# A fused feed-forward and attention block: in the first stage the two half products of a token tile walk together

## The reference

```python
x = x + 0.5 * ffn(layernorm(x))      # first layer
x = x + attention(layernorm(x))      # 32 heads, 8 key/value heads, per token
x = x + 0.5 * ffn(layernorm(x))      # third layer, the same weights

def ffn(x):                          # 1024 -> 1024, 64 centroids
    dots = softmax(x @ centroids.T / 0.1)
    hits = dots > 0.01
    query_sel, cluster_sel = any(hits, axis=1), any(hits, axis=0)
    dense = x @ weight.T + bias
    return where(query_sel[:, None] & cluster_sel[assignments][None, :], dense, 0)
```

## Time and profile before

| | us |
|---|---|
| median of 3 runs | 1223.47 (1221.32 to 1224.46) |
| span of the profiled execution, first to last instruction | 1220.6 |
| PE busy | 1207.2 (99%) |
| PE weight loads busy | 1039.3 (85%) |
| DVE busy | 858.3 (70%) |
| ACT busy | 412.6 (34%) |
| POOL busy | 420.5 (34%) |

### The profile page before, as it was taken

One profiled execution on the slowest core, in us unless ns is written; L12 is line 12 of the kernel. 1 busy time (PEld: TensorE's weight loads), 2 busy tenths in 40 slices (PEclk: granted clock), 3 DMA queues, 4 the chain that ended last, 5 costly groups with the idle time before them and its releaser, 6 DMA issues.

```text
span 1220.6 us, 21763 instructions
## 1 busy us (share of the span) xinstructions
PE 1207.2 (99%) x8536; PEld 1039.3 (85%) x8536; DVE 858.3 (70%) x1272; ACT 412.6 (34%) x590; POOL 420.5 (34%) x551
## 2 busy tenths in 40 slices
PE   7999999999999999999999999999999999999998
PEld 6888888888888888888888888888888888888887
DVE  6644654554463587888878888788888874289897
ACT  5322232222121234444444444444434443212120
POOL 1344445444226443233333333333233200050322
PEclk9999999999999999999999999999999999999999
DMA  8577767775754456555565555555555555117885
GB/s 275 148 198 243 200 196 208 226 205 163 202 135 167 110 132 177 148 153 136 156 164 139 153 151 154 156 140 159 135 169 141 137 151 183 38 54 248 302 288 194
DMA packets 318982, 208.54 MB, mean 171 GB/s; under 512 B 258336, under 2 KB 281632, under 8 KB 318880
## 3 DMA queue, kind: packets, MB, share of 16 engines
q1 hardware_dynamic: 303712, 187.74, 53.5%
q10 hardware_dynamic: 15168, 19.40, 4.7%
HBM read 118.49 MB, written 88.60 MB: 170 GB/s over the span
## 4 chain that ended last, share of the span: by engine, by line
PE 79%; DVE 7%; DMA 7%; issue 3%; SPq 2%; POOL 1%; ACT 1%; POOLq 0%; DVEq 0%; ACTq 0%
PE ps_b L276 12%; PE ps_b L278 12%; PE ps_b L277 12%; PE ps_a L276 9%; PE ps_a L278 9%; PE ps_a L277 9%; PE ps_t L283 5%; PE ps_s L1406 4%; PE ps_s L290 2%; DMA late<-x_scratch 2%; PE ps_s L292 2%; PE ps_s L1451 2%; DMA qkv_scratch<-qkv_tok 1%; DMA y_scratch<-xa 1%; DVE late L1188 1%
## 5 line engine op out<-in xcount | busy, mean ns | idle before, releaser
L276 PE MATMUL ps_a<-w_hi,odd_hi 128*128 128x512 f32 (+1 forms) x472 | 187.6, 397 | 0.0
L278 PE MATMUL ps_a<-w_hi,odd_lo 128*128 128x512 f32 (+1 forms) x472 | 183.5, 389 | 0.0
L277 PE MATMUL ps_a<-w_lo,odd_hi 128*128 128x512 f32 (+1 forms) x472 | 183.0, 388 | 0.0
L276 PE MATMUL ps_b<-proj_hi,y_hi 128*128 128x256 f32 (+1 forms) x512 | 177.7, 347 | 0.0
L278 PE MATMUL ps_b<-proj_hi,y_lo 128*128 128x256 f32 (+1 forms) x512 | 172.7, 337 | 0.0
L277 PE MATMUL ps_b<-proj_lo,y_hi 128*128 128x256 f32 (+1 forms) x512 | 172.0, 336 | 0.0
L309 POOL TENSOR_TENSOR var_eps<-moments,eps 128x1 f32<-128x1 f32 x96 | 18.4, 191 | 394.9 <-DVE moments L305 394.9
L684 POOL TENSOR_TENSOR x_ring<-x_ring,f_tmp 128x1024 f32<-128x1024 f32 x32 | 77.1, 2410 | 156.4 <-DVE probs L1139 112.7
L989 DVE TENSOR_TENSOR f_out<-ps_b,bias_a 128x512 f32<-128x512 f32 x30 | 20.7, 691 | 140.5 <-PE ps_b L278 140.4
L632 POOL TENSOR_SCALAR f_out<-f_out,token_on 128x1024 f32<-128x1024 f32 x30 | 85.6, 2855 | 75.8 <-DVE f_out L989 75.6
L278 PEld LDWEIGHTS ps_b<-proj_hi,y_lo 128*128 128x128 f32 x512 | 97.1, 190 | 10.8
(11 more groups left out here) (192 smaller groups left out, 2726.1 us busy)
## 6 DMA issues: line engine op xcount, KB each, us to landing
xa<-in_L_attn_x SPq DMA_DIRECT2D x32, 512.0 KB, 5.0
f_tmp<-f_scratch SPq DMA_DIRECT2D x32, 512.0 KB, 4.5
x_ring<-in_L_attn_x SPq DMA_DIRECT2D x32, 512.0 KB, 3.4
f_scratch<-f_out SPq DMA_DIRECT2D x30, 512.0 KB, 3.9
x_scratch<-x_ring SPq DMA_DIRECT2D x30, 512.0 KB, 3.2
y_scratch<-xa SPq DMA_DIRECT2D x28, 512.0 KB, 4.3
ya_tok<-y_scratch SPq DMA_DIRECT2D x112, 128.0 KB, 3.3
late<-x_scratch SPq DMA_DIRECT2D x22, 512.0 KB, 6.9
```

Source lines behind the costliest of these rows:

```text
L276: pe.matmul(acc, hi[:, k, :], w_h[:, k, cols], start=(k == 0), stop=False)
L277: pe.matmul(acc, hi[:, k, :], w_l[:, k, cols], start=False, stop=False)
L278: last = pe.matmul(acc, lo[:, k, :], w_h[:, k, cols], start=False, stop=(k == KB - 1))
```

## The change

A new function, `product_whole(t)`, does both halves of a tile in one walk over the 8 blocks. Each of the three stationary blocks of a step is used for half 0 and then for half 1, so that successive matmuls write two banks in turn, and the walk waits for both `f1_read[0]` and `f1_read[1]` before its first matmul. `ffn1[0]` is raised by the last matmul but one and `ffn1[1]` by the last. The walk takes the place of both halves for tiles 2p and 2p+1 with p from 2 to 12: 22 tiles, 1056 matmuls. The other tiles, and all other engines' programs, stay as they were.

```diff
+                def product_whole(t, between={}):
+                    hi, lo = first_set(t)
+                    acc = first_acc(t)
+                    pe.wait_ge(lo1, t + 1)
+                    for h in range(2):
+                        pe.wait_ge(f1_read[h], t - 1)
+                    for k in range(KB):
+                        if k in between:
+                            between[k]()
+                        for n, (x, w) in enumerate(((hi, w_hi), (hi, w_lo), (lo, w_hi))):
+                            for h in range(2):
+                                last = pe.matmul(acc[:, half(h)], x[:, k, :], w[:, k, half(h)],
+                                                 start=(k == 0 and n == 0), stop=(k == KB - 1 and n == 2))
+                                if k == KB - 1 and n == 2:
+                                    last.then_inc(ffn1[h], 1)
...
                 for p in range(1, NP - 2):
-                    product_first(2 * p, 0, {3 if p == 1 else 1: lambda: fold_pair(p)})
-                    product_first(2 * p, 1)
+                    if p == 1 or p == NP - 3:
+                        product_first(2 * p, 0, {3 if p == 1 else 1: lambda: fold_pair(p)})
+                        product_first(2 * p, 1)
+                    else:
+                        product_whole(2 * p, {1: lambda: fold_pair(p)})
                     if p > 1:
                         pair_first(p + 1)
-                    product_first(2 * p + 1, 0)
                     if p == 1:
+                        product_first(2 * p + 1, 0)
                         pair_first(p + 1)
-                    if p < NP - 3:
                         product_first(2 * p + 1, 1)
+                    elif p < NP - 3:
+                        product_whole(2 * p + 1)
+                    else:
+                        product_first(2 * p + 1, 0)
```

## The result

The changed kernel takes 1242.45 us (median of 4 runs, 1241.67 to 1242.68) against 1223.72 us of the kernel before; the ratio is 1.0156, with a 95% interval of 1.0141 to 1.0170. It is slower by 18.7 us. The profiled execution has a span of 1240.8 us and took 1242.68 us.

The account below looks back on a forecast made before the run. PE bounds the kernel as a nearly hole-free row of matmuls. Eleven later `pair_first`, 10 x 1.97 + 0.94 = 20.6 us, take the span from 1220.6 to 1241.2; 2.9 us around it give 1244 us, range 1230 to 1252.

Parts of the forecast that it names:

- The stream: PE's 1056 matmuls in the two-bank walk: the step stays 0.2265 us, 0 gained or lost by repeated block or bank change.
- The rivals with a faster stream: PE's matmul step gets shorter: 13.9 us back, 1230 us (chance 0.10), or enough to win, 1203 us (chance 0.04).
- the 131 ns of the Trainium skill: Skill's time per sustained 512-column matmul on PE; it would gain 101 us, but the prediction held the trace's 226.5 ns against it.
- The stall: PE at `pair_first`: low part queued behind DVE's late read, start 1.87 us later plus 0.10 us exposed weight load, 1.97 us each.
- The first of the eleven: First affected `pair_first`, behind tile 4, where PE already waited: starts at 84.75 instead of 83.81, 0.94 us more.
- The sum: First stage, eleven `pair_first` for p = 2 to 12: 10 x 1.97 + 0.94 = 20.6 us more.
- Behind the first stage: Later stages: PE waits for hardly anything, no wait could shrink, so the loss stays and everything shifts by 20 us.
- The span and what lies around it: Whole execution: span 1220.6 + 20.6 = 1241.2 us, plus 2.9 us around it as before, 1244 us.
- The 1.7 us to spare: ACT's high part ends at 154.62, low part not wanted before 156.30; a longer stall, 1252 us, had chance 0.09.
- The clock: Rival: PE's clock falls to 1.2 GHz for a tile after ten 1.7 us holes, 96 us, 1340 us; chance 0.03.

Follow-up runs that it names:

- the low part ahead of the read: The changed kernel with one swap on DVE, low part of tile 2p+3 before the read of half 0 of tile 2p: 1222.50 us, ratio 0.9999.
- the read ahead: The changed kernel with the read of half 1 of tile 2p also moved before the low part of tile 2p+3 on DVE: 1260.62 us, ratio 1.0310.
- the halves, again: Repeat of the kernel before with the pair's centroid product moved behind the sixth block of half 0 of tile 2p+1: 1221.97 us, ratio 0.9984.

## Why the prediction was right

The forecast was 1244 us, 20 us slower, and 1242.45 us was measured; the spans are 1241.2 forecast and 1240.8 measured. Step by step:

- **The stream.** Forecast: no gain from the repeated block, none from the change of bank. Shown: 0.2268 us a step after, as many weight loads, and equal times, to within their intervals, with the walk and without it once the signal is the same (1242.02 in halves, 1242.45 whole). The rivals with a faster stream fall, and with them the 131 ns of the Trainium skill ("TensorE: Matmul & The Clock Gate", "Back-to-back issue gap").
- **The stall.** Forecast 1.87 us per `pair_first` and 0.10 us for the exposed load; measured 1.86 us, and 0.22 us to the second matmul. DVE's read was forecast 0.02 us ahead of the end of the tile's last step and started 0.02 us ahead of it (161.14 against 161.16).
- **The first of the eleven.** Forecast 0.94 us more than before; measured 0.91 (from the centroid product ahead of it 20.36 us against 19.45).
- **The sum.** Forecast 20.6 us for the first stage. Measured between the third and the last centroid product: 323.49 us (64.97 to 388.46) against 302.67 (64.36 to 367.03), so 20.8. The 0.2 us that the sum lacks are a wait at the last centroid product, at 388.46, of a tile behind the changed ones, which was not considered: the row of its weight load shows 0.46 us idle, until L967.
- **Behind the first stage.** The prediction had the rest merely shifted. From the last centroid product to the end of the span it took 852.3 us against 853.6: 1.3 us less. The 1.9 us wait at 462 us, which the profile of before shows, is not in the profile after, which has one of 0.4 us at 918 us instead. No profile with a late report of the even tiles has that wait; the prediction counted on no wait that could shrink, and there was one. The medians too differ by 2.1 us less (18.7) than the first stage lost in the profiles (20.8).
- **The span and what lies around it.** The spans agree to 0.4 us, and that is in part luck: the third centroid product, ahead of every changed tile, already came 0.6 us later (64.97 against 64.36), the first stage lost 0.2 us more than forecast, and 1.3 us came back behind it. From span to time 2.9 us were given; in the recorded executions with both numbers it is 1.8 to 1.9. So about 1 us of the 2.9 is that the profiled execution of before was a short one of its kernel, and this and the 0.4 us are most of the 1.6 us by which 1244 came out high.
- **The 1.7 us to spare.** Held: in all eleven pairs the low part followed the read at once, without a wait for its turn or for ACT. In the pair shown the high part was ready 1.95 us ahead of it (159.80 and 161.75), where 1.7 was forecast. With the low part ahead of the read this spare time is gone, and some pairs waited for the DMA round trip.
- **The clock.** Given 0.03 and it did not fall, behind eleven holes of 1.7 us. The reason given was weak: one hole of 1.9 us without a fall. With the read ahead there is a hole of the same 1.9 us that has a fall behind it, while one of 2.3 us in the halves, again (at 461 us), has none. That none of the eleven of 1.7 us had one was right, by a margin that nobody knew then. The price of the rival was far off: a fall costs 1.5 us and not the 9.6 us of a whole tile. The change of bank moved the clock nowhere: with the low part ahead of the read all eleven executions show 1.00.

## What to carry to other kernels

When two results of an engine are reported together instead of one after the other, look at who reads the first, and at what stands behind that read on the reader's in-order queue: here a read moved by half a tile held up work that PE needed 0.22 us after it was ready. An engine that is 70% busy can still be without slack at one place of its order. The cheap repair, both ways of which brought the time back here, is to put what the bound engine waits for ahead of what only waits for the bound engine, or to give the bound engine other work first.

## What the runs showed of the hardware

- Using one 128x128 fp32r block for two matmuls running saves nothing inside the stream: each matmul has its own weight load of 188 ns, and the step is 0.2268 us in two alternating banks, 0.2265 us in one.
- The granted clock stayed at 1.00 (2.4 GHz) behind eleven holes of 1.7 us on PE in the profile, and its mean at 1.00 in all four executions. With eleven holes of 2.3 us and one of 1.9 us it went to 1.2 GHz for about 3 us behind 7 of the 12, every second one and the last, which is the one of 1.9 us; with one hole of 4.0 us and ten of 3.15 us behind 4 of these 11; each fall cost about 1.5 us. So the longer holes had fewer falls, and the time does not go up evenly with the hole: 0.6 us more per hole cost 18 us in all, another 0.9 us per hole only 5. The length of a hole alone does not decide it: the hole of 1.9 us in the kernel before had no fall, that of 2.3 us in the halves with the pair product inside had none, and one of four executions with holes of 3.15 us had none at all. What decides it is not shown here.
- Digits of the page that stand for 31 us each do not show falls of 3 us: the PEclk row is 9 in every slice of the profiles with 7 and with 4 falls. The mean granted clock (0.991 and 0.995) and the distances between rows show them.
